# Cross attention rewritten: a ring of transposed context chunks, and a convolution folded into the transposed probabilities

## The reference

```python
energy = jnp.einsum('bcn,bmn->bcm', x1, x2)          # x1 = layernorm(x), x2 = context
attn = jax.nn.softmax(energy, axis=-1)
attn = attn / (RENORM_EPS + attn.sum(axis=1, keepdims=True))
x_r = jnp.einsum('bcm,bmn->bcn', attn, x1_2)         # x1_2 = the same context
t = x1 - (jnp.einsum('oc,bcn->bon', conv_w, x_r) + conv_b[None, :, None])
t_bn = batch norm of t over the axes 0 and 2
return x1 + relu(t_bn)
```

## Time and profile before

| | |
|---|---|
| median of 3 runs | 1551.66 us (1548.22 to 1552.07) |
| profiled execution: time, span | 1551.59 us, 1549.6 us |
| mean granted clock of PE | 0.985 of full speed |
| cross attention, from the start to the first transpose after it (L800) | 586.16 us of the span |
| PE busy, share of the span | 96% |
| moved by DMA | 282.05 MB, 182 GB/s on average |

### The profile page before, as it was taken

The page is one execution under the profiler, slowest core; times in us unless marked ns, Lnnn a source line. Parts: engine busy times, 40 slices in busy tenths (PEclk is TensorE's granted clock), DMA queues, the critical chain, the costliest instruction groups (busy, mean ns, idle before and its releaser), DMA issues.

```text
span 1549.6 us, 17515 instructions
## 1 busy us (share of the span) xinstructions
PE 1486.6 (96%) x7178; PEld 708.8 (46%) x7178; DVE 769.4 (50%) x1272; ACT 425.9 (27%) x680; POOL 2.7 (0%) x12
## 2 busy tenths in 40 slices
PE   7999999999999878999999999999999999999995
PEld 3444535454453524444555555444444444444442
DVE  3434425352442437873777767655787762002006
ACT  2221314132131313212334444100566653000002
POOL 0000000000000000000000000000000000000000
PEclk9999999999999988999999999999999999999997
DMA  9895958669594667774444333122466651111112
GB/s 341 292 360 192 396 193 326 252 238 345 191 389 184 231 252 268 251 251 163 136 129 144 116 128 136 56 80 52 128 188 183 195 146 52 41 38 38 38 35 108
DMA packets 132207, 282.05 MB, mean 182 GB/s; under 512 B 40720, under 2 KB 57360, under 8 KB 132128
## 3 DMA queue, kind: packets, MB, share of 16 engines
q1 hardware_dynamic: 130256, 274.12, 50.9%
q10 hardware_dynamic: 1872, 6.82, 1.2%
HBM read 252.07 MB, written 28.84 MB: 181 GB/s over the span
## 4 chain that ended last, share of the span: by engine, by line
PE 78%; issue 15%; DVE 2%; SPq 2%; DMA 2%; ACT 1%; DVEq 0%; POOLq 0%; POOL 0%; ACTq 0%
PE ps L823 14%; PE ps L946 14%; PE ps L770 12%; PE ps L809 7%; PE ps L899 7%; PE ps L700 7%; PE ps L715 7%; PE ps L667 3%; SPq L315 2%; DMA ctxT<-in_ctx0T 1%; PE ps L780 1%; PE ps L845 1%; PE ps L756 1%; PE ps L703 1%; PE ps L863 1%
## 5 line engine op out<-in xcount | busy, mean ns | idle before, releaser
L823 PE MATMUL ps<-x2T,wqk_sb 128*128 128x512 f32 x512 | 224.1, 594 | 0.0
L959 PE MATMUL ps<-t_half,h_hi 128*128 128x512 f16 x512 | 194.0, 379 | 0.0
L959 PE MATMUL ps<-t_half,h_lo 128*128 128x512 f16 x512 | 194.0, 379 | 0.0
L770 PE MATMUL ps<-ctx_sb,attnT 128*64 128x512 f32 (+1 forms) x832 | 182.6, 599 | 0.0
L823 PEld LDWEIGHTS ps<-x2T,wqk_sb 128*128 128x128 f32 x512 | 95.6, 190 | 112.9 <-issue 112.4
L1032 DVE COPY ctxT<-ps 128x512 f32<-128x512 f32 (+1 forms) x128 | 83.7, 658 | 114.2 <-PE ps L700 96.8
L496 ACT ACTIVATE ctxT<-ps 128x512 f32<-128x512 f32 (+1 forms) x160 | 88.8, 579 | 187.1 <-PE ps L700 168.6
L700 PEld LDWEIGHTS ps<-cst,ctx_sb 128*128 128x128 f32 x1024 | 109.9, 140 | 53.7 <-issue 37.0
L700 PE MATMUL ps<-cst,ctx_sb 128*128 128x128 f32 x1024 | 130.3, 280 | 2.2 <-DMA ctx_sb<-in_ctx 2.2
L715 PE MATMUL ps<-ctxT,x1T 128*64 128x512 f32 x512 | 124.0, 605 | 0.0
L946 PE MATMUL ps<-x3h,t_buf 128*128 128x512 f16 x512 | 120.9, 379 | 0.0
(11 more groups left out here) (173 smaller groups left out, 1404.0 us busy)
## 6 DMA issues: line engine op xcount, KB each, us to landing
ctx_sb<-in_ctx SPq DMA_DIRECT2D x44, 2048.0 KB, 15.2
ctxT<-in_ctx0T SPq DMA_DIRECT2D x14, 2048.0 KB, 17.0
w_scan<-in_w1t SPq DMA_DIRECT2D x32, 512.0 KB, 5.0
w_buf<-in_w1t SPq DMA_DIRECT2D x32, 512.0 KB, 3.6
w_scan<-in_w2t SPq DMA_DIRECT2D x32, 512.0 KB, 4.5
t_dram<-t_out SPq DMA_DIRECT2D x64, 256.0 KB, 2.0
w_buf<-in_w2t SPq DMA_DIRECT2D x32, 512.0 KB, 3.8
ctx_sb<-in_ctx SPq DMA_DIRECT2D x16, 512.0 KB, 9.6
```

What stands on the lines that cost most here:

```text
L770: ins = mm(bank(2 + hf)[C * b:C * b + C, :], attnT[0:w, mt, C * b:C * b + C], ctx_sb[0:w, b, mt, hf * BANK:hf * BANK + BANK], start=(mt == ...
L823: ins = mm(bank(b0 + hf), wqk_sb[:, w, c, :], x2T[:, c, hf * BANK:hf * BANK + BANK], start=(c == 0), stop=(c == NC - 1))
L959: ins = mm(bank(t), part[:, t * P:t * P + P], t_half[:, hc % 8, :], start=(hc == 0 and n == 0), stop=(hc == HC - 1 and n == 1))
```

## The change

The same cross attention is written anew.

- The context's transposed form comes from memory for 896 columns instead of 512, that is for mt 0 to 6. It is laid out on the host in chunks: one for each 128 features, with both batches, 7168 bytes on each partition. A ring of eight slots (`ctxT`) holds them. `chunk_energies` computes the energies of one chunk in four matmuls, two of 512 and two of 384 columns.
- PE transposes mt 7 to 12 alone, in 12 pairs a tile: four transposes for batch 0 into bank 6, four for batch 1 into bank 7. ACT copies bank 6, DVE bank 7, to one of two staging buffers `stg`. mt 7 and mt 12 have two pairs each (half of the features each), mt 8 to 11 go together in eight "wide" pairs, one for each 128 features. In the first tile every row tile has pairs of its own.
- The rows of the context are loaded in five groups, both batches in one transfer, 8 KB in one piece. A load goes out when the weighting has finished with its group.
- The probabilities are no longer divided. DVE divides the convolution matrix by the sums instead (130 columns, `conv_s`: the matrix and two columns of ones over the sums), and PE multiplies the 13 blocks of probabilities with it (L724). That gives in one matmul the transposed block, the convolution and the column sums. The weighting result then needs no further matmul and no copy: DVE forms the residual from PSUM, half by half.
- x + x1 is not stored. `x` is read again and DVE forms the sum with one pass (`both`), from the mean and the root kept for each tile.
- The lambdas of the second attention are prepared inside the cross attention, and small inputs come in one transfer.

```diff
-STEPS = 4 * (G - 2) + 1
-U_X1, U_AT = 4 * STEPS, 4 * STEPS + 2
-UNITS = U_AT + G
-TB = 3
-USES = UNITS // TB
-assert UNITS % (2 * TB) == 0
-ORDER = (1, 2, 3, 0)
-LAST_ORDER = (0, 1, 3, 2)
+TM = 7
+TW = TM * P
+AW = P + 2
+SLOTS = 8
+
+N_GROUPS = ((7, 8), (9, 10), (11, 12), (0, 1, 2, 3), (4, 5, 6))
+PV_GROUPS = N_GROUPS
+LAST_GROUPS = ((0, 1, 2, 3), (6, 7, 8), (9, 10), (4, 5), (11, 12))
+G = len(N_GROUPS)
+UNITS = ((7, 8, 9), (10, 11, 0), (12,), (1, 2, 3), (4, 5, 6))
+LAST_UNITS = ((0, 1, 2), (3, 6, 7), (8, 9, 10), (4, 5, 11), (12,))
+U = len(UNITS)
+
+SINGLES = [(mt, half) for mt in range(TM, MT) for half in range(2)]
+PAIRS = SINGLES[:2] + [("wide", c) for c in range(NC)] + SINGLES[-2:]
+E = len(PAIRS)
+assert len(SINGLES) == E
...
+        ctxT = sb("ctxT", [P, SLOTS, 2, TW], 104 * KB)
+        stg = sb("stg", [P, 2, 2, BANK], 160 * KB)
...
+            def load_T(q, chunks):
+                for c in chunks:
+                    k = NC * q + c
+                    if k >= SLOTS:
+                        sp.wait_ge(ctxT_used, k - SLOTS + 1)
+                    sp.dma_start(ctxT[:, k % SLOTS, :, :], ctxT_in[q, c]).then_inc(ctxT_got[k % SLOTS], 16)
+
+            def load_N(q, g):
+                m0, m1 = N_GROUPS[g][0], N_GROUPS[g][-1] + 1
+                full = min(m1, MT - 1)
+                sp.dma_start(ctx_sb[:, m0:full, :, :], ctx[q, m0 * P:full * P].rearrange("(t p) b n -> p t b n", p=P))\
+                  .then_inc(ctx_in[g], 16)
+                if m1 == MT:
+                    sp.dma_start(ctx_sb[0:TAIL, MT - 1, :, :], ctx[q, full * P:M]).then_inc(ctx_in[g], 16)
...
+            load_T(1, range(0, 4))
+            load_N(0, 3)
+            load_N(0, 4)
+            load_T(1, range(4, NC))
+            for p in range(NT - 1):
+                if p + 2 < NT:
+                    load_T(p + 2, range(0, 4))
+                for g in range(G):
+                    sp.wait_ge(pv_done, G * p + g + 1)
+                    load_N(p + 1, g)
+                if p + 2 < NT:
+                    load_T(p + 2, range(4, NC))
...
+                sp.dma_start(xo[:, h4, :], x_v[h4].rearrange("t p n -> p t n")).then_inc(s_in[i], 16)
+            sp.wait_ge(pv_done, G * NT - 2)
+            sp.dma_start(wv_sb[:, :, :], wv.rearrange("(c p) n -> p c n", p=P)).then_inc(wv_in, 16)
...
+                    if E * p + e >= 2:
+                        act.wait_ge(e_done, E * p + e - 1)
+                    act.wait_ge(act_tr, pair_no(p, e) + 1)
+                    A(stg[:, e % 2, 0, 0:n], bank(6, n), ACT.Copy).then_inc(act_tr_out, 1)
+                    if e == 2 and p + 1 < NT:
+                        sqrt(p + 2, slice(0, 1))
+                    if e == 8 and p + 2 < NT:
+                        load_x(p + 2)
...
+                A(prob[:, 0:2 * BANK], ps[:, ea * BANK:(ea + 2) * BANK], ACT.Exp, bias=nmx[:, 0:1], accum_out=zs[:, 0:1])\
...
+            def chunk_energies(q, chunks):
+
+                ea = 4 * (q % 2)
+                for c in chunks:
+                    k = NC * q + c
+                    pe.wait_ge(ctxT_got[k % SLOTS], 16 * (k // SLOTS) + 16)
...
+                    for g, (m0, m1) in enumerate(((0, BANK), (BANK, TW))):
+                        for b in range(2):
+                            ins = mm(bank(ea + g, m1 - m0)[C * b:C * b + C, :], x1T[:, q % 2, c, C * b:C * b + C],
+                                     ctxT[:, k % SLOTS, b, m0:m1], start=(c == 0), stop=(c == NC - 1))
+                    ins.then_inc(ctxT_used, 1)
...
+            def pair_transposes(p, e):
+                kind, a = pairs(p)[e]
+                n = pair_no(p, e)
+                if e == 0:
+                    pe.wait_ge(ctx_in[0], 16 * p + 16)
+                    if p:
+                        pe.wait_ge(at_out, U * p)
+                if e in (2, 4):
+                    pe.wait_ge(ctx_in[1], 16 * p + 16)
+                    pe.wait_ge(ctx_in[2], 32 * p + 32)
+                for b, (s_out, s) in enumerate(((act_tr_out, act_tr), (dve_tr_out, dve_tr))):
...
+                    for i in range(4):
+                        if kind == "wide":
+                            ins = pe.transpose(bank(6 + b)[:, i * P:i * P + P], ctx_sb[:, 8 + i, b, a * P:a * P + P], ident)
...
+            def pairs_of(p):
+                for e in range(1, E):
+                    pair_transposes(p, e)
+                    if e < E - 1:
+                        pair_energies(p, e - 1)
+                pair_energies(p, E - 2)
+                if p + 1 < NT:
+                    put_x1T(p + 1)
+                pair_energies(p, E - 1)
...
+            def weights_T(p):
+
+                units = UNITS if p < NT - 1 else LAST_UNITS
+                pe.wait_ge(exp_done, 2 * p + 2)
+                pe.wait_ge(aug_ready, p + 1)
...
+                for u, mts in enumerate(units):
+                    if u == U - 1:
+                        pe.wait_ge(at_out, U * p + 1)
+                    for i, mt in enumerate(mts):
+                        w = width(mt)
+                        ins = mm(bank(unit_bank(u))[0:w, i * AW:i * AW + AW], prob[:, mt * P:mt * P + w], conv_s[:, :],
+                                 start=True, stop=True)
+                    ins.then_inc(at_ready, 1)
...
+                            ins = mm(bank(ea + hf)[C * b:C * b + C, :], attnT[0:w, slots[mt], C * b:C * b + C],
+                                     ctx_sb[0:w, mt, b, hf * BANK:hf * BANK + BANK], start=(mt == order[0]), stop=(mt == order[-1]))
+                        if mt == order[-1] and hf == 0:
+                            ins.then_inc(pv_half, 1)
+                    ins.then_inc(pv_done, 1)
...
-                        ins = pe.transpose(bank(5 + (u_at + n) % TB)[0:w, i * P:i * P + P], prob[:, m0:m0 + w], ident)
...
-                for hf, s in enumerate((xr_act, xr_dve)):
-                    pe.wait_ge(s, p + 1)
-                    mm(bank(4 if hf == 0 else par), conv_bd[:, :], xr_sb[:, hf * BANK:hf * BANK + BANK], start=True, stop=True)\
-                        .then_inc(cv_done, 1)
...
+            for p in range(NT):
+                if p + 1 < NT:
+                    chunk_energies(p + 1, range(0, 4))
+                weights_T(p)
+                weigh_ctx(p)
+                if p + 1 < NT:
+                    chunk_energies(p + 1, range(4, NC - 1))
+                    pair_transposes(p + 1, 0)
+                    chunk_energies(p + 1, range(NC - 1, NC))
+                    pairs_of(p + 1)
...
+                for hf, (s, n) in enumerate(((pv_half, p + 1), (pv_done, G * p + G))):
+                    V.wait_ge(s, n)
+                    tt = x1s[:, p % 2, hf * BANK:hf * BANK + BANK]
+                    V.scalar_tensor_tensor(tt, bank(4 * (p % 2) + hf), cols[:, 0:1], tt, ALU.add, ALU.subtract)\
+                        .then_inc(cv_free, 1)
...
+                for e, pair in enumerate(pairs(p)):
+                    n = BANK if pair[0] == "wide" else 4 * width(pair[0])
+                    if E * p + e >= 2:
+                        V.wait_ge(e_done, E * p + e - 1)
+                    V.wait_ge(dve_tr, pair_no(p, e) + 1)
+                    V.tensor_copy(stg[:, e % 2, 1, 0:n], bank(7, n)).then_inc(dve_tr_out, 1)
+                    if e == 0 and p + 1 < NT:
+                        stats(p + 1)
+                    if e == 4:
+                        V.wait_ge(e_done, E * p + 2)
+                        own.done(V.tensor_reduce(mx4[:, 0:1], ps[:, ea * BANK:(ea + 2) * BANK], AX.X, ALU.max))
+                    if e == 6 and p + 1 < NT:
+                        make_x1(p + 1)
...
-                o.done(V.tensor_tensor(zs[:, 2:3], zs[:, 0:1], zs[:, 1:2], ALU.add))
-                o.done(V.reciprocal(cs[:, 0:1], zs[:, 2:3]))
-                V.tensor_scalar(prob[:, :], prob[:, :], cs[:, 0:1], None, ALU.mult).then_inc(attn_ready, 1)
...
-                    o.done(V.tensor_reduce(c, t, AX.X, ALU.add))
-                    o.done(V.tensor_scalar(c, c, 1e-9, None, ALU.add))
-                    o.done(V.reciprocal(c, c))
-                    V.tensor_tensor(attnT[0:n, 4 * g:4 * g + nt, :].rearrange("p t (b c) -> p (t b) c", c=C), t,
...
-                V.tensor_copy(xr_sb[:, BANK:2 * BANK], bank(3)).then_inc(xr_dve, 1)
...
+                V.tensor_scalar(conv_s[:, :], conv_bd, zs[:, 2:3], None, ALU.mult).then_inc(aug_ready, 1)
...
+                    V.wait_ge(at_ready, U * p + u + 1)
+                    t = bank(unit_bank(u), nt * AW)[0:n, :].rearrange("p (t a) -> p t a", a=AW)
+                    c = cs[0:n, u, 0:nt, :]
+                    own.done(V.tensor_scalar(c, t[:, :, P:AW], 1e-9, None, ALU.add))
+                    own.done(V.reciprocal(c, c))
+                    s = slots[mts[0]]
+                    V.tensor_tensor(attnT[0:n, s:s + nt, :].rearrange("p t (b c) -> p t b c", c=C),
+                                    t[:, :, 0:P].rearrange("p t (b c) -> p t b c", c=C),
```

(3 more changed lines are left out.)

616 lines of the change are left out of this document (237 added, 379 removed).

## The result

The changed kernel takes 1509.92 us, the median of 4 runs (1509.63 to 1511.94), beside 1550.39 for the kernel before (4 runs, 1548.22 to 1552.07): ratio 0.9743, 95% interval 0.9726 to 0.9759. The forecast was 1512. The profiled execution took 1509.63 with a span of 1507.8 us.

The account below looks back on a forecast made before the run. PE's instruction issue, start to start, was taken as the bound. Gains of 1 (tile 0), 31.1 (six tiles), 7.0 (last tile) and 1.1 (batch norm) make 40.2 off 1551.59: 1511.4, stated as 1512 us; eight-in-ten range 1503 to 1526.

Parts of the forecast that it names:

- The tile in the middle: Each of six tiles between first and last: 63.0 us against 68.18, 31.1 us won in all.
- the 0.2 for switches of bank: Part of the 3.4 us for multiplying probabilities with the convolution (L724): 3.2 for 26 records, 0.2 for bank switches.
- the 0.5 added for DVE's other work: Allowance per middle tile for DVE's other pieces delaying a copy between pairs, raising 62.5 us to 63.0.
- 48 transposes are 6.0: In a middle tile, the transposes taken from PE, at 0.124 us each, win 6.0 us.
- the prediction's own check: Middle tile counted by differences: 8.3 us won (transposes, L780, wait), 3.1 lost (convolution in blocks, switches, mt 7 split).
- Tile 0: First tile: its weighting ends at 93 us instead of 94.24, a gain of 1 us.
- at 400 GB/s and 3 us for start and landing that is 36.5 us: Start of tile 0: 13.3 MB must arrive before the third pair, taking 36.5 us, or 41 at 350 GB/s.
- Last tile: Final cross-attention tile: 60.3 us against 67.32, 7.0 won, with an exposed wait of 3.2.
- The cost of the low clock: In the last tile, placed in the weighting, taken as 24.7 us as before, at 0.89 of the clock.
- Batch norm: After the last weighting: one copy and the convolution gone, DVE gains under 1.2 us of work, net 1.1 less.
- Transfers as the bound: Rival, 8%: below 341 GB/s transfers set the tile; at 330, 7 tiles lose 3 us each, giving 1533.
- Two banks: Rival, 9% together with a slower-than-before case: pairs take 2.25 us, the tile loses 2.8, giving about 1534.

Follow-up runs that it names:

- e5: The changed kernel without the chunk loads of tiles 1 to 7, the first tile's chunks standing in: 1509.57 us, ratio 0.9731.
- e3: The changed kernel with four PSUM banks in turn for the pairs instead of two: 1510.01 us, ratio 0.9737.
- e1: The changed kernel with 512 context columns from memory instead of 896, mt 4 to 7 transposed on PE in wide pairs: 1566.76 us, ratio 1.0099.
- e9: The changed kernel with division, transposes and convolution separate again, the fourth chunk's energies before the last block of probability transposes: 1518.01 us, ratio 0.9785.
- e13: The changed kernel loading 128 rows in place of the last 65 in every tile: 1509.65 us, ratio 0.9735.
- e10: The changed kernel with four next-tile chunks loaded behind the rows of mt 7 to 12, for two tiles, tile 0's waits kept: 1506.73 us, ratio 0.9720.
- e4: The changed kernel with each row group of tile 0 waited for only where it is used: 1512.92 us, ratio 0.9750.
- e8: The changed kernel with e4's waits, and four chunks of tile 2 loaded behind the rows of mt 7 to 12 of tile 1: 1503.63 us, ratio 0.9686.
- e6: The changed kernel with one more 4.2 MB memory-to-memory transfer in each of the first seven tiles: 1533.74 us, ratio 0.9887.

## Why the prediction was right, and where it was off

**The bound.** Right: PE's instructions start to start. Less traffic (e5) and more banks (e3) leave the tile at 62.15 to 62.3.

**The tile in the middle.** The sum of the parts was 62.5, measured 62.33. Wide pair 2.02, measured 2.03; chunks 12.4 for eight, measured 12.42; L724 3.4, now 3.10: a record costs 0.119 start to start, less than the 0.122 of the earlier trace rows, and the 0.2 for switches of bank was not needed. The term that was mis-sized is the 0.5 added for DVE's other work: the timeline of a tile shows no wait for a copy of `stg`. It makes 3 of the 4 us by which the six tiles beat the forecast. The other 1 is the 0.17 a tile by which the parts were too dear: L724 by 0.3 and the weighting by 0.1, less 0.2 that the pairs and the transposes of `x1` cost more.

**What the gain consists of.** The step "48 transposes are 6.0" is borne out by e1 (6.5 a tile, with the switches that go too). The convolution in the blocks brings 0.5 to 0.8 a tile by e9, where the prediction's own check had 0.2 (1.8 for L780, 1.6 back), with a wait of 0.5 besides. The new form of the rest costs about what it saves: with 512 columns it is at 68.86 against 68.18.

**Tile 0.** Wrong in its sign: its weighting ends at 97.40, 4.4 us behind the 93. The step is "at 400 GB/s and 3 us for start and landing that is 36.5 us". The bytes kept to it: by the windows some 13.8 MB had been moved at 36 us, which is what the load has with all ahead of it (not 13.3: the 705 rows are 5.8 MB). Yet the third pair started at 42.02, when 15.3 MB had been moved. So the step that failed is that a load has landed when its bytes and those ahead of it have been moved. What the trace shows in its place is a load that lands in parts, and a wait that ends with the last of them: the first of the parts for mt 11 and 12 landed at 36.10, the last at 41.93, and in between bytes of later loads were moved. In the slow stretch packets of 8 KB take 0.54 us instead of 0.32; but in e13, without it, one part was still 1.7 us behind all others. Why one part is so late, and why this differs between executions (the last part at 39.13 in e10, at 43.66 in e5), stays open. In e10 the stretch also ended earlier: 421 GB/s from 39 to 42 us, where e5 had 215.

The rest of the sum for tile 0 fits: from the third pair's start to the weighting's end it gave 56.3, and 55.4 were measured. What I did not ask is whether the wait was needed: e4 and e8 show that it is not, but that it pays to take it away only when the loads behind it are in the order of use.

**Last tile.** The wait is 3.35 (forecast 3.2). The cost of the low clock was placed wrongly: it fell on L724 (4.72 start to start instead of 3.10), and the weighting ran in 22.5, not 24.7. The first error is 1.3, the second 2.2 the other way; with 0.5 more for pairs, chunks and the wait, the piece comes out 0.3 us under its 60.3. That is luck, since the place where the clock costs was not foreseen.

**Batch norm.** 1.8 won instead of 1.1. Ahead of the small matmul (L766, before L791) 2.2 are won, as forecast (from the weighting's end 4.92 us before, to the line below, and 2.68 after); behind it 0.4 are lost (10.61 to 11.02), where the three short operations and the first pass (`both`) had been put at up to 1.2.

```profile
575.55 0.38 PE L791 MATMUL ps<-bnm,cst 128*128 128x2 f32 x2 [2.93 <-DVE bnm L1093]
```

**The total.** The forecast of 1512 (the sum gave 1511.4) is 2.1 us from the median because the pieces err both ways: tile 0 is 4.2 worse than forecast, the six tiles 4.0 better, the last tile, the batch norm and all that follows together 1.8 better. The tile in the middle was understood to 0.7 us of 62.3; that the sum is as near as it is, is in part luck. In the profiles of e3 and e10 the earlier start alone moved the time by some 3 us.

**The rivals.** Transfers as the bound: the place from which it decides, 341 GB/s, was right for the demand (343 to 348 measured), and e6 shows what the queue gave when asked for more, 391 on average; after has 420 from 42 to 60 us. The Trainium skill (DMA: Bandwidth & Descriptors, Where 436 GB/s comes from) has about 358 GB/s for a core as the limit of loads from HBM; the traces disagree here too, with these 420. Two banks: e3 shows no effect.
